# A recurrent cell on one core: the order of the second half's scan and z transpose on VectorE, and of its tanh and update gate on ScalarE

## The chip, the cores and the metric

The kernel runs on one core of one Trainium2 chip. The metric is device time in microseconds (us), the median of several runs, each of the whole program. A core has five engines that run side by side and wait for one another by semaphores: TensorE (PE, and PEld for its weight loads), VectorE (DVE), ScalarE (ACT), GpSimd (POOL) and SyncE (SP), which issues transfers.

## What is computed

A gated recurrent cell runs over T = 512 time steps for a batch of 8, with 512 inputs and 512 latent units, all in float32:

```python
def step(h, x_t):
    fused = sigmoid(concatenate([x_t, h], -1) @ w_W + w_b)
    r, z = split(fused, 2, axis=-1)                 # reset gate, update gate
    m = x_t @ wx_W + wx_b + r * (h @ wh_W + wh_b)   # memory_state
    h_new = z * h + (1.0 - z) * tanh(m)
    return h_new, h_new
out = x + scan(step, h0, x)
```

Each step needs the h of the step before, so the 512 steps form one chain.

## The kernel before

**Tiling.** The 512 latent units are KC = 4 chunks of 128 and are worked on as two halves, `o = 0` and `o = 1`, of two chunks each. On TensorE the 8 columns of h (one for each of the batch) are the stationary operand and the weights stream past, 64 columns to a product; four column tiles of 32 stand side by side. So the products of h land in PSUM with the batch on partitions and have to be turned by VectorE (`transpose` in blocks of 32) before they meet h again.

**TensorE, one step** (lines 325 to 353). The products are ordered by which half of h they need: `r(0)`, `m(0)`, `z(0, 0)` take the first half of h and wait for `h_ready[0]` (line 327); then `products_of_parts(0)` (bf16 thirds of h, which make r and m of the second half in one bank, "rm"); then line 339 waits for `h_ready[1]`, and `r(1)`, `m(1)`, `z(0, 1)` follow (48 products), `products_of_parts(1)` (24), which ends with `rm_done`, `z(1, 0)` and `z(1, 1)` (32 products, ended by `z_done[1]`), and last 8 wide products of x for a later step, `x_products` (line 265), which depend on no h of this step.

**VectorE, one step** (`step`, lines 468 to 501), in the order in which its queue takes them: turn r, m and z of the first half (434, 437, 444); `mix_m(0)`, a scan that makes r * m + x (453); `turn_rm` (441) after `rm_done`; `sum_parts(0)` (447), which gives r of the second half; `mix_h(0)`, the scan that makes the first half of the new h (461); `sum_parts(1)` (447), which gives m of the second half and signals `m_summed`; `turn_z(1)` (444), which signals `z_turned[1]`; `mix_m(1)` (453), which waits for `r_ready[1]`, `x_moved` and `m_summed` (490 to 492) and signals `m_pre_ready[1]`; `mix_h(1)` (461), which waits for `tanh_ready[1]` and `z_ready[1]` and signals `h_ready[1]`. After every fourth step a 384-wide `add_bias` follows (466).

**ScalarE, one step** (lines 384 to 405): sigmoid of r (368), sigmoid of z (375, `update(0)`), tanh (381, `new(0)`), all of the first half; the copy `put_first` (357) that puts biases and x products into PSUM for the next step; sigmoid of the second half's r (372), `put_rm` (361); then `update(1)` (375), `new(1)` (381), and `put_z` (365).

**GpSimd, one step** (lines 573 to 583): `x_moved` (576), the two subtractions that cut each half of the new h into bf16 thirds and end in `parts_ready` (544, 546), and the sum of h and x for the output (554). SyncE only moves x, the partial products `ahead` and the output.

The order on each engine is written out by hand. Every engine takes its instructions in that order, and a wait holds back all that stands behind it on the same engine.

Of the kernel before, what the change touches and what calls it, by code (L numbers as in the profile page):

```python
# [14 lines left out]
def build(nc, x, h0, w_h, w_x, b_x, b_h, x_rows, out):  # L15
# [49 lines left out]
    with ctx:  # L65
# [6 lines left out]
        def halves(name):  # L72
            return [sem(f"{name}{o}") for o in range(HALVES)]
# [82 lines left out]
        z_done = halves("z_done")  # L156
# [3 lines left out]
        z_turned = halves("z_turned")  # L160
# [10 lines left out]
        z_ready = halves("z_ready")  # L171
        m_pre_ready = halves("m_pre_ready")
        tanh_ready = halves("tanh_ready")
# [9 lines left out]
        def held(eng, value):  # L183
            return value if isinstance(value, int) else eng.snap(value)
# [169 lines left out]
        @block.scalar  # L354
        def _(act):
            def put_first(slot, t):
                act.activation(ps[:, 0:GATES, 0:W], ahead[:, slot, t, 0:GATES * W].rearrange("p (g n) -> p g n", n=W),  # L357
                               ACT.Copy).then_inc(first_ahead, 1)

            def put_rm(slot, t):  # L360
                act.activation(ps[:, RM_BANK, 0:2 * W], ahead[:, slot, t, RM_AT:COLS], ACT.Copy).then_inc(rm_ahead, 1)  # L361

            def put_z(slot, t):
                at = Z_AT[1]
                act.activation(ps[:, Z_BANK[1], 0:W], ahead[:, slot, t, at:at + W], ACT.Copy).then_inc(z_ahead, 1)

            def reset_first():
                act.activation(m_by[:, 0, :, 1].rearrange("p (c b) -> p c b", b=B), turned_r[:, :, 0:B], ACT.Sigmoid)\  # L368
                    .then_inc(r_ready[0], 1)

            def reset_second():
                act.activation(m_by[:, 1, :, 1], summed[:, 0, :, 0], ACT.Sigmoid).then_inc(r_ready[1], 1)  # L372

            def update(o):
                act.activation(h_by[:, o, :, 2].rearrange("p (b c) -> p c b", c=HC), turned_z[:, o, :, 0:B], ACT.Sigmoid)\  # L375
                    .then_inc(z_ready[o], 1)

            def new(o, s):
                n_twice = h[:, (s - 1) % RING, o, 1:1 + REGION].rearrange("p (b c w) -> p c b w", c=HC, w=TRI)[:, :, :, 0::2]
                pre = m_pre[:, o, :, 1].rearrange("p (c b) -> p c b", b=B)  # L380
                act.activation(n_twice, pre.unsqueeze(3).to_broadcast([P, HC, B, 2]), ACT.Tanh)\  # L381
                    .then_inc(tanh_ready[o], 1)

            def step(i, t0, s):
                nxt = held(act, t0 + (s + 1))
                slot, t = (s + 1) // RING % SLOTS, (s + 1) % RING
                if t == 0:
                    turn = held(act, (i * (PER_BLOCK // SLOTS) + ((s + 1) // RING // SLOTS + 1)) * LANDED)
                act.wait_ge(r_turned, nxt)
                reset_first()  # L390
                act.wait_ge(z_turned[0], nxt)
                update(0)
                act.wait_ge(m_pre_ready[0], nxt)
                new(0, s)
                if t == 0:
                    act.wait_ge(ahead_loaded[slot], turn)
                put_first(slot, t)
                act.wait_ge(r_summed, nxt)
                reset_second()
                put_rm(slot, t)  # L400
                act.wait_ge(z_turned[1], nxt)
                update(1)
                act.wait_ge(m_pre_ready[1], nxt)
                new(1, s)
                put_z(slot, t)

            act.dma_start(bias_x[:, :], b_x).then_inc(bias_x_loaded, 16)
            act.dma_start(bias_h[:, :, :], b_h).then_inc(bias_h_loaded, 16)
            act.dma_start(h_0[:, :, :], h0).then_inc(h0_loaded, 16)
            act.wait_ge(start_h, 1)  # L410
            act.activation(warm[:, :], h[:, 0, 0, 0:Q], ACT.Sigmoid)
            act.wait_ge(x_biased, 1)
            act.wait_ge(bias_h_put, HALVES)
            put_ahead(act, 0, 16)
            for k in range(KC):
                act.wait_ge(rest_once, k + 1)
                act.activation(w_parts[:, k, 1], w_rest[:, k], ACT.Copy).then_inc(second_cut, 1)  # L417
            for k in range(KC):
                act.wait_ge(rest_twice, k + 1)
                act.activation(w_parts[:, k, 2], w_rest[:, k], ACT.Copy).then_inc(third_cut, 1)  # L420
            act.wait_ge(bits_set, 1)
            act.wait_ge(ahead_loaded[0], LANDED)
            put_first(0, 0)
            put_rm(0, 0)
            put_z(0, 0)
            with nc.Fori(0, BLOCKS, engines=(mybir.EngineType.Activation,), hint_back_edge=True) as i:
                t0 = act.snap(i * STEPS)
                for s in range(STEPS):
                    step(i, t0, s)

        @block.vector
        def _(dve):
            def turn_r():
                return dve.transpose(turned_r[:, :, :], ps[:, R_BANK, 0:W].rearrange("p (c q) -> p c q", q=Q))  # L434

            def turn_m():
                return dve.transpose(turned_m.rearrange("p g (c b) w -> p c g w b", b=B),  # L437
                                     ps[:, M_BANK, 0:W].rearrange("p (c q) -> p c q", q=Q))

            def turn_rm():  # L440
                return dve.transpose(turned_rm[:, :, :], ps[:, RM_BANK, 0:2 * W].rearrange("p (c q) -> p c q", q=Q))  # L441

            def turn_z(o):
                return dve.transpose(turned_z[:, o], ps[:, Z_BANK[o], 0:W].rearrange("p (c q) -> p c q", q=Q))  # L444
# [6 lines left out]
            def mix_m(o, add):  # L451

                return dve.tensor_tensor_scan(m_pre[:, o].rearrange("p i w -> p (i w)"),  # L453
                                              m_by[:, o].rearrange("p i w -> p (i w)"),
                                              add.rearrange("p i w -> p (i w)"), 0.0, ALU.mult, ALU.add)

            def mix_h(o, s, nxt):

                dve.wait_ge(tanh_ready[o], nxt)
                dve.wait_ge(z_ready[o], nxt)  # L460
                dve.tensor_tensor_scan(h[:, s % RING, o, 0:REGION], h_by[:, o].rearrange("p i w -> p (i w)"),  # L461
                                       h[:, (s - 1) % RING, o, 1:1 + REGION], 0.0, ALU.mult, ALU.add)\
                    .then_inc(h_ready[o], 1)
# [4 lines left out]
            def step(i, t0, s):  # L468
                nxt = held(dve, t0 + (s + 1))
                dve.wait_ge(r_done, nxt)  # L470
                if s % 2 == 0:

                    dve.wait_ge(y_added, held(dve, t0 + (s + STEPS - RING + 2)))
                turn_r().then_inc(r_turned, 1)
                dve.wait_ge(m_done, nxt)
                turn_m().then_inc(m_turned, 1)
                dve.wait_ge(z_done[0], nxt)
                turn_z(0).then_inc(z_turned[0], 1)
                dve.wait_ge(r_ready[0], nxt)
                dve.wait_ge(m_turned, nxt)  # L480
                mix_m(0, turned_m[:, 0]).then_inc(m_pre_ready[0], 1)
                dve.wait_ge(rm_done, nxt)
                turn_rm().then_inc(rm_turned, 1)
                dve.wait_ge(rm_turned, nxt)
                sum_parts(0).then_inc(r_summed, 1)
                mix_h(0, s, nxt)
                sum_parts(1).then_inc(m_summed, 1)
                dve.wait_ge(z_done[1], nxt)
                turn_z(1).then_inc(z_turned[1], 1)
                dve.wait_ge(r_ready[1], nxt)  # L490
                dve.wait_ge(x_moved, nxt)
                dve.wait_ge(m_summed, nxt)
                mix_m(1, summed[:, 1]).then_inc(m_pre_ready[1], 1)
                mix_h(1, s, nxt)
                if s % RING == RING - 1:

                    g = s // RING
                    dve.wait_ge(x_product, held(dve, i * PER_BLOCK + (g + 3)))
                    dve.wait_ge(ahead_loaded[(g + 1) % SLOTS],
                                held(dve, (i * (PER_BLOCK // SLOTS) + ((g + 1) // SLOTS + 1)) * LANDED))  # L500
                    add_bias(X_BANK)
# [138 lines left out]
```

## Time and profile before

| what | value |
|---|---|
| median of 3 runs | 1635.45 us (1634.96 to 1636.28) |
| the profiled execution | 1634.35 us, of which the trace's span is 1632.2 us |
| mean granted TensorE clock | 0.995 of full speed |
| PE busy | 1603.5 us (98%) |
| DVE busy | 1162.8 us (71%) |
| ACT busy | 910.0 us (56%) |
| POOL busy | 682.3 us (42%) |
| steps | 512, so 3.1 us each |

The profile is that of one execution. "Busy" is the time in which an engine has an instruction under way. TensorE's records overlap (its matmuls are pipelined, and their ends are modelled), so there the distance from one start to the next tells more than the durations. The same is true, in a smaller way, on VectorE and ScalarE: an instruction's record may begin before the record ahead of it has ended.

### The profile page before, as it was taken

Reading aid. Unit: us, or ns where it says so; the run is one execution under the profiler, and the core shown is the slowest. Engines: PE = TensorE matmul, PEld = TensorE weight load, DVE = VectorE, ACT = ScalarE, POOL = GpSimd, SP = SyncE. Lnnn points to the kernel's source line nnn. Section 1 sums busy time; section 2 is a strip of 40 time slices with the busy share of each in tenths; the row PEclk is TensorE's granted clock in tenths of the full one; section 3 lists DMA queues with packets and bytes.
Section 4 is the critical chain, followed back from the end, with each engine's and each line's share of the span. In section 5 each row is a group of like instructions: output and inputs, shape, how many; then the busy total and the mean of one; then the engine's idle time right before and its main releaser. Section 6 shows DMA issues by size and latency. Waiting matters only on the chain.

```text
span 1632.2 us, 213115 instructions
## 1 busy us (share of the span) xinstructions
PE 1603.5 (98%) x94336; PEld 1377.4 (84%) x94336; DVE 1162.8 (71%) x5782; ACT 910.0 (56%) x4621; POOL 682.3 (42%) x3084
## 2 busy tenths in 40 slices
PE   5899999999999999999999999999999999999998
PEld 3788888888888888888888888888888888888887
DVE  3677777777777777777777777777777777777776
ACT  2455555555555555555555555555555555555555
POOL 1344444444444444444444444444444444444443
PEclk7999999999999999999999999999999999999999
DMA  6111111111111111111111111111111111111111
GB/s 203 31 51 48 52 37 49 47 53 50 47 39 51 49 47 54 37 47 52 51 48 48 40 50 47 52 51 47 39 50 50 47 53 38 48 52 50 49 47 41
DMA packets 194891, 83.29 MB, mean 51 GB/s; under 512 B 123200, under 2 KB 194368, under 8 KB 194880
## 3 DMA queue, kind: packets, MB, share of 16 engines
q1 hardware_dynamic: 193824, 82.47, 18.7%
q10 hardware_dynamic: 1056, 0.67, 0.2%
q8 instruction: 6, 0.10, 0.0%
q14 instruction: 5, 0.04, 0.0%
HBM read 49.30 MB, written 33.75 MB: 51 GB/s over the span
## 4 chain that ended last, share of the span: by engine, by line
PE 97%; DMA 1%; issue 0%; ACT 0%; ACTq 0%; DVE 0%; SPq 0%; POOL 0%; POOLq 0%; DVEq 0%
PE ps L274 56%; PE ps L283 21%; PE ps L265 20%; DMA wx<-in_w_x 1%; DMA x_rows<-xs_biased 0%; ACTq L198 0%; ACT w_parts L417 0%; ACTq L194 0%; ACT w_parts L420 0%; SPq L211 0%; SPq L209 0%; DVE xs_biased L466 0%; DVE h L461 0%; DVE turned_rm L441 0%; POOL y L554 0%
## 5 line engine op out<-in xcount | busy, mean ns | idle before, releaser
L274 PE MATMUL ps<-wh,h 128*8 128x64 f32 x65536 | 1218.0, 219 | 20.0 <-ACT ps L357 14.6
L274 PEld LDWEIGHTS ps<-wh,h 128*8 128x8 f32 x65536 | 1030.9, 92 | 238.8 <-DVE h L461 216.4
L283 PE MATMUL ps<-w_parts,h 128*24 128x128 bf16 x24576 | 544.1, 219 | 0.0
L283 PEld LDWEIGHTS ps<-w_parts,h 128*24 128x24 bf16 x24576 | 442.8, 121 | 0.0
L265 PE MATMUL ps<-wx,x_grp 128*32 128x384 f32 x4096 | 430.7, 486 | 0.0
L368 ACT ACTIVATE m_by<-turned_r 128x16 f32<-128x16 f32 x512 | 112.0, 219 | 561.4 <-DVE turned_r L434 561.4
L544 POOL TENSOR_TENSOR h<-h 128x16 f32<-128x16 f32 x1026 | 224.4, 219 | 365.5 <-DVE h L461 361.9
L461 DVE TENSOR_TENSOR_SCAN h<-h_by,h 128x48 f32<-128x48 f32 x1024 | 260.6, 254 | 160.9 <-ACT h L381 160.9
L576 POOL TENSOR_TENSOR summed<-turned_rm,nothing 128x16 f32<-128x16 f32 x512 | 113.5, 222 | 498.6 <-DVE turned_rm L441 498.6
L434 DVE STREAM_TRANSPOSE turned_r<-ps 128x64 f32<-128x64 f32 x512 | 128.1, 250 | 262.9 <-PE ps L274 258.4
L375 ACT ACTIVATE h_by<-turned_z 128x16 f32<-128x16 f32 x1024 | 238.5, 233 | 117.9 <-DVE turned_z L444 63.2
L546 POOL TENSOR_TENSOR h<-h 128x16 f32<-128x16 f32 x1026 | 225.0, 219 | 80.4
L381 ACT ACTIVATE h<-m_pre 128x32 f32<-128x32 f32 x1024 | 252.7, 247 | 0.0
L444 DVE STREAM_TRANSPOSE turned_z<-ps 128x64 f32<-128x64 f32 x1024 | 247.9, 242 | 2.9 <-PE ps L274 2.9
L447 DVE TENSOR_REDUCE summed<-turned_rm 128x16 f32<-128x48 f32 x1024 | 197.1, 192 | 17.4
L357 ACT ACTIVATE ps<-ahead 128x192 f32<-128x192 f32 x513 | 171.6, 335 | 0.0
L441 DVE STREAM_TRANSPOSE turned_rm<-ps 128x128 f32<-128x128 f32 x512 | 162.1, 317 | 0.3 <-PE ps L283 0.3
L554 POOL TENSOR_TENSOR y<-x_sb,h 128x32 f32 x512 | 137.9, 269 | 0.9
L361 ACT ACTIVATE ps<-ahead 128x128 f32<-128x128 f32 x513 | 135.1, 263 | 0.0
L437 DVE STREAM_TRANSPOSE turned_m<-ps 128x64 f32<-128x64 f32 x512 | 119.5, 233 | 1.5 <-PE ps L274 1.4
L372 ACT ACTIVATE m_by<-summed 128x16 f32<-128x16 f32 x512 | 112.1, 219 | 14.5 <-DVE summed L447 0.4
L453 DVE TENSOR_TENSOR_SCAN m_pre<-m_by,summed 128x32 f32<-128x32 f32 x512 | 115.0, 225 | 0.0
(29 smaller groups left out, 429.4 us busy)
## 6 DMA issues: line engine op xcount, KB each, us to landing
x_rows<-xs_biased SPq DMA_DIRECT2D x128, 192.0 KB, 1.9
ahead<-x_rows SPq DMA_DIRECT2D x512, 32.0 KB
ahead<-x_rows SPq DMA_DIRECT2D x1024, 8.0 KB
x_sb<-in_x SPq DMA_DIRECT2D x34, 256.0 KB, 3.1
x_grp<-in_x SPq DMA_DIRECT2D x516, 16.0 KB, 1.7
out_h<-y SPq DMA_DIRECT2D x32, 256.0 KB, 2.7
wx<-in_w_x SPq DMA_DIRECT2D x4, 768.0 KB, 9.1
wh<-in_w_h SPq DMA_DIRECT2D x4, 512.0 KB, 7.3
```

Source lines behind the costliest of these rows:

```text
L265: mm = pe.matmul(ps[Q * j:Q * (j + 1), bank, 0:COLS], stands, wx[:, k, j, :], start=(k == 0), stop=(k == KC - 1), tile_position=(0, Q * j))
L274: mm = pe.matmul(ps[Q * j:Q * j + B, bank, 0:W], h_of(s - 1, k), wh[:, k, j, at:at + W], start=False, stop=(k == KC - 1), skip_group_check ...
L283: mm = pe.matmul(ps[Q * j:Q * j + PARTS * B, RM_BANK, 0:2 * W], parts_of(s - 1, k), w_parts[:, k, part, j], start=False, stop=(k == KC - 1 ...
L357: act.activation(ps[:, 0:GATES, 0:W], ahead[:, slot, t, 0:GATES * W].rearrange("p (g n) -> p g n", n=W), ACT.Copy).then_inc(first_ahead, 1)
L375: act.activation(h_by[:, o, :, 2].rearrange("p (b c) -> p c b", c=HC), turned_z[:, o, :, 0:B], ACT.Sigmoid)\
L381: act.activation(n_twice, pre.unsqueeze(3).to_broadcast([P, HC, B, 2]), ACT.Tanh)\
L441: return dve.transpose(turned_rm[:, :, :], ps[:, RM_BANK, 0:2 * W].rearrange("p (c q) -> p c q", q=Q))
L444: return dve.transpose(turned_z[:, o], ps[:, Z_BANK[o], 0:W].rearrange("p (c q) -> p c q", q=Q))
L447: return dve.tensor_reduce(summed[:, g, :, 0].rearrange("p (c b) -> p c b", b=B), turned_rm[:, HC * g:HC * (g + 1)].rearrange("p c (w b) - ...
L461: dve.tensor_tensor_scan(h[:, s % RING, o, 0:REGION], h_by[:, o].rearrange("p i w -> p (i w)"), h[:, (s - 1) % RING, o, 1:1 + REGION], 0.0 ...
L544: pool.tensor_tensor(mid(1, s, o), mid(0, s, o), mid_top(0, s, o), ALU.subtract).then_inc(left_once[o], 1)
L546: pool.tensor_tensor(mid(2, s, o), mid(1, s, o), mid_top(1, s, o), ALU.subtract)\
```

## The change

It moves one instruction on each of two engines and swaps two waits. On VectorE, `mix_m(1)` with its three waits now stands directly behind `sum_parts(1)`, and `turn_z(1)` with its wait for `z_done[1]` behind `mix_m(1)`. On ScalarE, the second half's tanh `new(1)` with its wait for `m_pre_ready[1]` now stands ahead of the sigmoid `update(1)` with its wait for `z_turned[1]`. In `mix_h(1)` the wait for `z_ready[1]` is now written first and that for `tanh_ready[1]` second; `mix_h(0)` keeps its order. No instruction is added, removed or resized, and TensorE, GpSimd and SyncE have the same code.

```diff
@@ ScalarE step
                 put_rm(slot, t)
+                act.wait_ge(m_pre_ready[1], nxt)
+                new(1, s)
                 act.wait_ge(z_turned[1], nxt)
                 update(1)
-                act.wait_ge(m_pre_ready[1], nxt)
-                new(1, s)
                 put_z(slot, t)
@@ VectorE mix_h(o, s, nxt)
-                dve.wait_ge(tanh_ready[o], nxt)
-                dve.wait_ge(z_ready[o], nxt)
+                for ready in ((tanh_ready[o], z_ready[o]), (z_ready[o], tanh_ready[o]))[o]:
+                    dve.wait_ge(ready, nxt)
@@ VectorE step
                 sum_parts(1).then_inc(m_summed, 1)
-                dve.wait_ge(z_done[1], nxt)
-                turn_z(1).then_inc(z_turned[1], 1)
                 dve.wait_ge(r_ready[1], nxt)
                 dve.wait_ge(x_moved, nxt)
                 dve.wait_ge(m_summed, nxt)
                 mix_m(1, summed[:, 1]).then_inc(m_pre_ready[1], 1)
+                dve.wait_ge(z_done[1], nxt)
+                turn_z(1).then_inc(z_turned[1], 1)
                 mix_h(1, s, nxt)
```

## Rows read from the trace of the kernel before

**Rows 1.** The page's chain that ended last: its shares by engine.
```profile
PE 97%; DMA 1%; issue 0%; ACT 0%; ACTq 0%; DVE 0%; SPq 0%; POOL 0%; POOLq 0%; DVEq 0%
```

**Rows 2.** Waits from 60 to 1600 us: who waited for whom, total us, times, longest.
```profile
PEld ps L274 <- DVE h L461: 211.5, 497, 0.4
DVE h L461 <- ACT h L381: 155.9, 496, 0.3
```

**Rows 3.** Timeline, PE: start us, us, engine, line, operation, idle before.
```profile
802.17 0.76 PEld L274 LDWEIGHTS ps<-wh,h 128*8 128x8 f32 x48 [0.42 <-DVE h L461]
802.25 0.87 PE L274 MATMUL ps<-wh,h 128*8 128x64 f32 x48
...
802.87 0.43 PEld L283 LDWEIGHTS ps<-w_parts,h 128*24 128x24 bf16 x24
...
803.21 0.73 PEld L274 LDWEIGHTS ps<-wh,h 128*8 128x8 f32 x48
...
803.87 0.43 PEld L283 LDWEIGHTS ps<-w_parts,h 128*24 128x24 bf16 x24
803.93 0.53 PE L283 MATMUL ps<-w_parts,h 128*24 128x128 bf16 x24
...
804.21 0.52 PEld L274 LDWEIGHTS ps<-wh,h 128*8 128x8 f32 x32
```

**Rows 4.** Timeline of the same step, DVE and ACT, the second half's work.
```profile
801.75 0.21 DVE L447 TENSOR_REDUCE summed<-turned_rm 128x16 f32<-128x48 f32 x1
...
801.87 0.25 DVE L461 TENSOR_TENSOR_SCAN h<-h_by,h 128x48 f32<-128x48 f32 x1
801.99 0.22 ACT L372 ACTIVATE m_by<-summed 128x16 f32<-128x16 f32 x1
802.04 0.18 DVE L447 TENSOR_REDUCE summed<-turned_rm 128x16 f32<-128x48 f32 x1
...
802.14 0.23 DVE L444 STREAM_TRANSPOSE turned_z<-ps 128x64 f32<-128x64 f32 x1
...
802.35 0.23 DVE L453 TENSOR_TENSOR_SCAN m_pre<-m_by,summed 128x32 f32<-128x32 f32 x1
802.41 0.23 ACT L375 ACTIVATE h_by<-turned_z 128x16 f32<-128x16 f32 x1
...
802.61 0.25 ACT L381 ACTIVATE h<-m_pre 128x32 f32<-128x32 f32 x1
...
802.89 0.26 DVE L461 TENSOR_TENSOR_SCAN h<-h_by,h 128x48 f32<-128x48 f32 x1 [0.32 <-ACT h L381]
```

**Rows 5.** Timeline, the same reduce and scan one step on.
```profile
805.15 0.18 DVE L447 TENSOR_REDUCE summed<-turned_rm 128x16 f32<-128x48 f32 x1
...
805.46 0.23 DVE L453 TENSOR_TENSOR_SCAN m_pre<-m_by,summed 128x32 f32<-128x32 f32 x1
```

**Rows 6.** Timeline, DVE alone, an early step: z's transpose came late, all else was ready.
```profile
40.08 0.25 DVE L444 STREAM_TRANSPOSE turned_z<-ps 128x64 f32<-128x64 f32 x1 [1.11 <-PE ps L274]
...
40.25 0.18 DVE L453 TENSOR_TENSOR_SCAN m_pre<-m_by,summed 128x32 f32<-128x32 f32 x1
```

**Rows 7.** Timeline, DVE, the first half's transposes and scan, then the next transpose.
```profile
804.00 0.21 DVE L437 STREAM_TRANSPOSE turned_m<-ps 128x64 f32<-128x64 f32 x1
804.11 0.22 ACT L368 ACTIVATE m_by<-turned_r 128x16 f32<-128x16 f32 x1 [1.13 <-DVE turned_r L434]
804.18 0.25 DVE L444 STREAM_TRANSPOSE turned_z<-ps 128x64 f32<-128x64 f32 x1
804.36 0.23 DVE L453 TENSOR_TENSOR_SCAN m_pre<-m_by,turned_m 128x32 f32<-128x32 f32 x1
...
804.50 0.32 DVE L441 STREAM_TRANSPOSE turned_rm<-ps 128x128 f32<-128x128 f32 x1
```

**Rows 8.** Lines from 60 to 1600 us: busy us, mean ns | idle before.
```profile
L444 DVE STREAM_TRANSPOSE turned_z<-ps 128x64 f32<-128x64 f32 x994 | 240.5, 242 | 0.0
L375 ACT ACTIVATE h_by<-turned_z 128x16 f32<-128x16 f32 x994 | 231.5, 233 | 109.6 <-DVE turned_z L444 56.2
```

## The prediction

> **What bounds the kernel now.** I read the chain that ended last first. It gives PE 97% [rows 1], so TensorE, which looks busy without a break, sets the time. Work that is moved between VectorE and ScalarE can then gain only what TensorE loses by waiting, and can cost whatever makes TensorE wait. So the question is how close each half of h arrives to the moment at which TensorE wants it. The waits name both places. The weight loads waited 211.5 us, 497 times, for the scan of line 461 [rows 2]: that is the first half, once a step. But it is PEld that waits; the wide x products run on meanwhile, and r(0)'s first matmul begins 0.08 us after its load (802.17 to 802.25), against 0.06 at the start of the parts block at 803.87 [rows 3]. The first half of h thus has a few hundredths of slack.
>
> The second half is what the change touches. Its scan on line 461 begins at 802.89 and lasts 0.26, so it ends at 803.15 [rows 4], and the load for r(1) begins at 803.21 [rows 3], 0.06 later. Is that load held up by h, or by the 24 loads ahead of it? From the first of those loads to the load of r(1) it is 802.87 to 803.21 = 0.34, and the same block of the other half, which has no h to wait for behind it, also takes 803.87 to 804.21 = 0.34 [rows 3]. So h's second half arrives just as TensorE is ready for it. A gain on it buys at most 0.01 us a step, the resolution of these rows, hence 5 us in 512 steps. A loss is paid nearly in full, since this is a loop: r(1), m(1), z(0,1) and parts(1) lead to `rm_done`, that to VectorE's turning and sums, and these to the second half of the next h. With that loop exactly as long as TensorE's own step, any time added on it lengthens every step.
>
> **What ends the second half now.** From the timeline [rows 4]: the sum of m, 802.04 + 0.18 = 802.22; the transpose of z, 802.14; the scan of m, 802.35; the sigmoid of z, 802.41; tanh, 802.61; the scan of h, 802.89. The last link is tanh (802.86), 0.03 ahead of that scan, and the waits say the same: line 461 waited for line 381 496 times, 155.9 us [rows 2]. Sigmoid ended at 802.64, 0.22 us earlier. From the start of the scan of m to the start of the scan of h it is 802.89 - 802.35 = 0.54.
>
> **The change part by part.** All 512 steps have it; nothing is added.
>
> 1. The scan of m is put ahead of the transpose of z. How much earlier does it begin? By the order of the queue alone, VectorE could give it 0.10 to 0.21. But its inputs bound it: r's sigmoid ends at 801.99 + 0.22 = 802.21 and the sum of m at 802.22 [rows 4]. The best case is 0.03 behind the latter, 802.25, as the scan of h follows tanh: 0.10 earlier. The worst is that nothing is gained. I choose the worst, from this: the scan begins 0.13 behind the end of that sum, and one step later again 805.15 + 0.18 = 805.33 to 805.46 = 0.13 [rows 4, 5]. The transpose between them doesn't explain this. Where everything else had long been ready, the same scan began 0.17 behind the transpose (40.08 to 40.25) [rows 6]; here it is 802.14 to 802.35 = 0.21, and its record is 0.23 long instead of 0.18 [rows 4, 6], as that of the scan at 804.36, which came just as its sigmoid ended (804.33) [rows 7]. So it is not queueing behind the transpose; it is being released late, and its releaser is the sum. It has three waits, and `m_summed` is the last in the code. As I read the 0.13, that wait has to pass by itself before the scan is taken up, and this costs the 0.10 over the 0.03. That path (sum, wait, scan) is the same in the changed kernel. The scan stays at 802.35, or moves by 0.02.
>
> The Trainium skill, "Perfetto Trace Analysis", section "Identifying Dependency Chains", says that an instruction with several waits may have separate wait instructions put ahead of it, and "Advanced Engine Details and Errata", "Network/Comms", gives 50-100 ns for a sequencer on TRN2 to read a semaphore. The 0.10 between 0.13 and 0.03 in the rows is of that size; no row shows such an instruction by itself.
>
> 2. The transpose of z now follows the scan. It was ready long before (z(1,1) is on TensorE ahead of the x products), so only the queue holds it. Spacing on VectorE: 0.14 behind a 0.23 scan of this form (804.36 to 804.50) [rows 7], where the next also waited for TensorE's block at 803.93 + 0.53 = 804.46 [rows 3], so 0.14 is an upper end; the lower is 0.10, as the transpose behind the 0.18 sum [rows 4]. I take 0.14, as records that overlap lie about 0.08 less than the duration apart in both pairs (0.18 and 0.10; 0.25 and 0.18 at 804.18 [rows 4, 7]). It lasts 0.23 [rows 4] to 0.25 [rows 7]; mean 0.242 [rows 8]. I take 0.24.
>
> 3. The sigmoid of z comes 0.04 behind the transpose's end (802.37 to 802.41), lasts 0.233, and the scan of h follows by 0.03 [rows 4, 8]. Tanh starts where it does now, 802.61, so ScalarE is free for the sigmoid in good time, though their records overlap. Behind the sigmoid, line 365's copy is later by as much; what it fills is wanted by z(1,0), at 804.2 + the delay, more than a microsecond on.
>
> 4. The swapped waits of `mix_h(1)`: the late one is again the one written first (tanh before, now z), so I take the same 0.03, not the 0.13 of the scan of m. In the code that is all that the swap does.
>
> **The sum.** From the start of the scan of m to that of h: 0.14 + 0.24 + 0.04 + 0.23 + 0.03 = 0.68, against 0.54 now: 0.14 later. Tanh, 0.22 late behind sigmoid now, is no longer the last; z is. Less 0.01 or nothing of slack: 0.13 a step. 512 x 0.13 = 66.6 us, on the profiled 1634.35: 1701.0. The median stands 1.1 above the profiled execution, so 1702 us, 4.1% slower. Ends: 0.10 + 0.23 + 0.03 + 0.23 + 0.03 = 0.62, with the scan 0.02 earlier and 0.01 slack, adds 0.05, 26 us (1661); 0.14 + 0.25 + 0.04 + 0.24 + 0.04 = 0.71 adds 0.17, 87 us (1722); these need all errors at once, so 1680 to 1716 for the case alone.
>
> Nothing else takes it back: TensorE's delayed r(1) delays `rm_done`, and every engine's step with it; GpSimd's cut of the second half starts from the same scan and shifts equally. SyncE's transfers are not on the path.
>
> **Rivals.**
> - *The scan of m does start 0.10 earlier*, at 802.25. For it: its inputs allow this. Against it: the 0.13 twice over and the long record. Then 0.14 - 0.10 = 0.04, less slack 0.03 to 0.04: 15 to 20 us, 1652.
> - *The chain of z is longer still*: the transpose starts only when the scan has ended (0.23 instead of 0.14), or the scan of h pays 0.10 for its late wait. 0.23 a step, 118 us: 1753. Against: 0.17 and 0.18 between 0.25 records [rows 6, 7]. The Trainium skill, "VectorE: DVE Perf Modes", "The DRAIN you can't avoid", has a next operation wait until the pipe is empty; the rows show overlap, as its own section on instructions with no wait between them allows.
> - *No change*, 1636: h's second half has 0.14 of slack that I don't see, since TensorE's ends are modelled. Against: its load starts 0.06 behind the end of the scan (803.15), and that of the first half, which is known to wait, 0.05 behind its own (801.87 + 0.25 = 802.12) [rows 3, 4].
> - *Faster*, the other side: the scan of m comes more than 0.15 earlier (the transpose sets its release after all, and the sum's signal comes ahead of its recorded end). It decides from a scan of m at 802.20: then 0.68 behind it is 802.88, before today's 802.89, and TensorE gets at most its 0.01 a step, 5 us: 1630. But 802.20 lies ahead of both inputs as recorded.
> - *TensorE's clock falls* in the new pauses of 0.13 us; it is 0.995 of the full 2.4 GHz on average with the present ones. At 1.2 GHz a step's 3.1 us of matmuls would double. I see no row for it.
>
> **How the numbers follow.** Forecast case 0.75, scan earlier 0.12, longer chain 0.04, no change 0.04, faster 0.04, clock 0.01. The range takes the forecast's own 1680 to 1716 and reaches down over the first rival, 1650 to 1716. About 0.2% is what a measurement of this kernel can tell from no change, so faster 0.04, same 0.04, slower 0.92.
>
> **What would show it.** In the changed trace: line 461 waits for line 375 instead of 381, 512 times; the scan of m still 0.13 behind the end of the sum; the transpose 0.14 behind the scan's start; the scan of h 0.68 behind it; a gap of 0.13 ahead of r(1) on PE and PEld, with a step of 3.23 us in place of 3.10; PE's share of the last chain down, with DVE and ACT in it. A scan of m 0.03 behind the sum would make it the first rival, an unbroken TensorE the third.

## The result, and the profile after

The changed kernel takes 1678.07 us (median of 5, 1677.77 to 1679.15), the kernel before 1635.45 (median of 5, 1634.52 to 1636.28). The ratio is 1.026, 95% interval 1.025 to 1.027: 42.6 us slower, or 42.6 / 512 = 0.083 us a step. The forecast was 1702, within 1650 to 1716.

| | before | after |
|---|---|---|
| profiled execution, its span | 1634.35, 1632.2 us | 1678.07, 1676.2 us |
| mean granted TensorE clock | 0.995 | 0.995 |
| PE busy | 1603.5 us | 1646.0 us |
| DVE busy | 1162.8 us | 1161.8 us |
| ACT busy | 910.0 us | 871.4 us |

The page of the changed kernel still gives nearly everything to TensorE. Its chain that ended last, shares by engine:

```profile
PE 97%; DMA 1%; issue 0%; ACT 0%; ACTq 0%; DVE 0%; SPq 0%; POOL 0%; DVEq 0%; POOLq 0%
```

That is the same 97% as in [rows 1], in a kernel that is slower although TensorE's instructions are the same. The prediction had expected the share to fall; it doesn't, so a share of 97% can't tell whether TensorE waits a little in every step. It falls only to 92% in `e3` and 91% in `e2` (below), where the block of r(1) comes on average 0.15 and 0.20 us later behind the one ahead of it than in the kernel before. The waits from 60 to 1640 us do show what has changed (total us, times, longest):

```profile
DVE h L461 <- ACT h_by L375: 149.1, 496, 0.3
ACT h L381 <- DVE m_pre L453: 121.7, 496, 0.4
```

The scan of h waited for tanh, line 381, in [rows 2]; now it waits for the sigmoid of z, line 375. And ScalarE stands idle ahead of tanh, since the sigmoid that used to fill this time is behind it. One step of the changed kernel, VectorE and ScalarE, answering to [rows 4]:

```profile
800.94 0.21 DVE L447 TENSOR_REDUCE summed<-turned_rm 128x16 f32<-128x48 f32 x1
...
801.24 0.18 DVE L447 TENSOR_REDUCE summed<-turned_rm 128x16 f32<-128x48 f32 x1
...
801.55 0.22 DVE L453 TENSOR_TENSOR_SCAN m_pre<-m_by,summed 128x32 f32<-128x32 f32 x1
...
801.70 0.22 DVE L444 STREAM_TRANSPOSE turned_z<-ps 128x64 f32<-128x64 f32 x1
801.81 0.25 ACT L381 ACTIVATE h<-m_pre 128x32 f32<-128x32 f32 x1 [0.24 <-DVE m_pre L453]
801.95 0.23 ACT L375 ACTIVATE h_by<-turned_z 128x16 f32<-128x16 f32 x1
...
802.22 0.26 DVE L461 TENSOR_TENSOR_SCAN h<-h_by,h 128x48 f32<-128x48 f32 x1 [0.30 <-ACT h_by L375]
```

The scan of m begins 801.55 - 801.42 = 0.13 behind the end of the sum, exactly as before: moving it ahead of the transpose gained nothing. The transpose of z is pushed from ahead of the scan to 0.15 behind its start, and z is now last: from the scan of m to the scan of h 0.67 us, against 0.54. TensorE in the same step, answering to [rows 3]:

```profile
802.08 0.42 PEld L283 LDWEIGHTS ps<-w_parts,h 128*24 128x24 bf16 x24
802.13 0.52 PE L283 MATMUL ps<-w_parts,h 128*24 128x128 bf16 x24
...
802.53 0.69 PEld L274 LDWEIGHTS ps<-wh,h 128*8 128x8 f32 x48
802.53 0.86 PE L274 MATMUL ps<-wh,h 128*8 128x64 f32 x48
...
803.21 0.52 PE L283 MATMUL ps<-w_parts,h 128*24 128x128 bf16 x24
```

From the first load of the parts block to the first load of r(1) it is 0.45 us, against 0.34 before, and between their first matmuls 0.40 (802.13 to 802.53), against 0.34 (802.92 to 803.26): that is the pause. Averaged over the steps from 60 to 1600 us the distance between these first matmuls is 0.409 us against 0.335, and that from r(1) to `products_of_parts(1)` 0.680 against 0.670: together the 0.08 a step that the change costs. The other four distances between blocks are the same in both kernels. The second thing to see is that r(1)'s first matmul starts together with its load (both 802.53). In the kernel before it started 0.05 behind it (803.21 in [rows 3]; the matmul is the last row below, from the timeline of that kernel). The load used to run 0.05 ahead of a matmul that still had other matmuls in front of it. That lead is the cover that the prediction did not count, and it is why the pause in this step is 0.11 between loads and 0.06 between matmuls. The kernel before, PE, in order `products_of_parts(1)`, z(1, 0) and z(1, 1), x, `products_of_parts(0)` and r(1):

```profile
800.83 0.53 PE L283 MATMUL ps<-w_parts,h 128*24 128x128 bf16 x24
801.16 0.64 PE L274 MATMUL ps<-wh,h 128*8 128x64 f32 x32
...
801.61 0.84 PE L265 MATMUL ps<-wx,x_grp 128*32 128x384 f32 x8
...
802.92 0.53 PE L283 MATMUL ps<-w_parts,h 128*24 128x128 bf16 x24
...
803.26 0.87 PE L274 MATMUL ps<-wh,h 128*8 128x64 f32 x48
```

### The profile page after: what moved, and what is told of

It reads as the page before. It is cut to its first block, busy times and chain, and to the rows that moved or that the text cites. A ratio compares the mean times of both kernels' runs of the same rounds, so it can differ in the third digit from the quotient of the medians.

```text
span 1676.2 us, 213115 instructions
## 1 busy us (share of the span) xinstructions
PE 1646.0 (98%) x94336; PEld 1396.8 (83%) x94336; DVE 1161.8 (69%) x5782; ACT 871.4 (52%) x4621; POOL 682.2 (41%) x3084
## 4 chain that ended last, share of the span: by engine, by line
PE 97%; DMA 1%; issue 0%; ACT 0%; ACTq 0%; DVE 0%; SPq 0%; POOL 0%; DVEq 0%; POOLq 0%
PE ps L274 57%; PE ps L283 20%; PE ps L265 20%; DMA wx<-in_w_x 1%; DMA x_rows<-xs_biased 0%; ACTq L198 0%; ACT w_parts L417 0%; ACT w_parts L420 0%; ACTq L194 0%; SPq L211 0%; SPq L209 0%; DVE xs_biased L466 0%; DVE h L461 0%; DVE m_pre L453 0%; DVE turned_rm L441 0%
## 5 line engine op out<-in xcount | busy, mean ns | idle before, releaser
L274 PE MATMUL ps<-wh,h 128*8 128x64 f32 x65536 | 1205.4, 220 | 20.3 <-ACT ps L357 14.3
L274 PEld LDWEIGHTS ps<-wh,h 128*8 128x8 f32 x65536 | 997.4, 92 | 262.3 <-DVE h L461 224.0
L283 PE MATMUL ps<-w_parts,h 128*24 128x128 bf16 x24576 | 532.0, 219 | 0.0
L283 PEld LDWEIGHTS ps<-w_parts,h 128*24 128x24 bf16 x24576 | 431.3, 121 | 0.0
L265 PE MATMUL ps<-wx,x_grp 128*32 128x384 f32 x4096 | 425.4, 487 | 0.0
L444 DVE STREAM_TRANSPOSE turned_z<-ps 128x64 f32<-128x64 f32 x1024 | 242.3, 237 | 3.2 <-PE ps L274 3.2
```

Source lines behind the costliest of these rows:

```text
L265: mm = pe.matmul(ps[Q * j:Q * (j + 1), bank, 0:COLS], stands, wx[:, k, j, :], start=(k == 0), stop=(k == KC - 1), tile_position=(0, Q * j))
L274: mm = pe.matmul(ps[Q * j:Q * j + B, bank, 0:W], h_of(s - 1, k), wh[:, k, j, at:at + W], start=False, stop=(k == KC - 1), skip_group_check ...
L283: mm = pe.matmul(ps[Q * j:Q * j + PARTS * B, RM_BANK, 0:2 * W], parts_of(s - 1, k), w_parts[:, k, part, j], start=False, stop=(k == KC - 1 ...
```

## The experiments

The working measure is one distance, read on VectorE: from the start of the first line-447 sum (of r, second half) to the start of the second half's scan of h. In the kernel before it is 1.15 us on average (1.14 in the step of [rows 4], 801.75 to 802.89). How much a kernel lengthens it, the delay, is compared with what a step costs, the difference of medians over 512.

### Each half of the change alone

`e1_scalar_only`: ScalarE's order and the swapped waits; VectorE as before.

```diff
                 put_rm(slot, t)
+                act.wait_ge(m_pre_ready[1], nxt)
+                new(1, s)
                 act.wait_ge(z_turned[1], nxt)
                 update(1)
-                act.wait_ge(m_pre_ready[1], nxt)
-                new(1, s)
```

> ScalarE's part alone: tanh ahead of the sigmoid of z, and the swapped waits of the scan of h; VectorE in the order of before. The scan of m stays 0.13 behind the sum, tanh starts where it did, the sigmoid 0.13 behind it: the scan of h 0.11 later. Theory A (0.05 of cover): 0.06 a step, 33 us, 1669. Theory B (0.01): 51 us, 1687.

Measured: 1663.5 us, ratio 1.018 (1.016 to 1.019), 28.5 us slower. The sigmoid of z, which ran 0.06 behind the start of the scan of m in [rows 4], now stands behind tanh and runs 0.40 behind it:

```profile
800.04 0.23 DVE L453 TENSOR_TENSOR_SCAN m_pre<-m_by,summed 128x32 f32<-128x32 f32 x1
...
800.30 0.25 ACT L381 ACTIVATE h<-m_pre 128x32 f32<-128x32 f32 x1 [0.23 <-DVE m_pre L453]
800.44 0.22 ACT L375 ACTIVATE h_by<-turned_z 128x16 f32<-128x16 f32 x1
...
800.69 0.26 DVE L461 TENSOR_TENSOR_SCAN h<-h_by,h 128x48 f32<-128x48 f32 x1 [0.42 <-ACT h_by L375]
```

ScalarE's new order costs on its own: with only that, 0.65 us from scan to scan.

`e2_vector_only`: VectorE's order; ScalarE and the waits as before.

```diff
                 sum_parts(1).then_inc(m_summed, 1)
-                dve.wait_ge(z_done[1], nxt)
-                turn_z(1).then_inc(z_turned[1], 1)
 ...
                 mix_m(1, summed[:, 1]).then_inc(m_pre_ready[1], 1)
+                dve.wait_ge(z_done[1], nxt)
+                turn_z(1).then_inc(z_turned[1], 1)
```

> VectorE's part alone: the scan of m ahead of z's transpose; ScalarE and the waits of the scan of h as before. Tanh has to stand behind the sigmoid of z, which waits for the late transpose: scan of h 0.29 later. Theory A: 0.24 a step, 123 us, 1758. Theory B: 0.28, 143 us, 1779. If the scan of m came 0.10 earlier through the move, both would be 51 us less.

Measured: 1742.7 us, ratio 1.066 (1.064 to 1.067), 107.6 us slower, more than the whole change. Tanh, whose input is ready, has to stand behind a sigmoid that waits for the late transpose. So VectorE's part is the larger loss, and ScalarE's part is what repairs most of it; together they cost 42.6. The delay was 0.25 rather than the 0.29 worked out. Neither half gains anything.

### The two waits of the scan of h

`e3_old_waits`: the changed kernel, tanh's wait written first again.

```diff
-                for ready in ((tanh_ready[o], z_ready[o]), (z_ready[o], tanh_ready[o]))[o]:
-                    dve.wait_ge(ready, nxt)
+                dve.wait_ge(tanh_ready[o], nxt)
+                dve.wait_ge(z_ready[o], nxt)
```

> The changed kernel, with the waits of the second scan of h in their old order (tanh written first, z second), so that the late one is the second. If the late wait costs 0.10 more where it is not the one written first, as the 0.13 behind the sum of m suggests: 51 us more than the changed kernel, 1729. If the order of the two waits means nothing: 1678.

Measured: 1714.1 us, ratio 1.049 (1.047 to 1.050), 36 us more than the changed kernel. The order in which two waits are written matters: the late one is cheap where it is written first.

```profile
801.92 0.23 ACT L375 ACTIVATE h_by<-turned_z 128x16 f32<-128x16 f32 x1
...
802.26 0.26 DVE L461 TENSOR_TENSOR_SCAN h<-h_by,h 128x48 f32<-128x48 f32 x1 [0.37 <-ACT h_by L375]
```

The scan starts 0.11 behind the sigmoid's end (802.15), in the changed kernel 0.04 (802.18 to 802.22). The price is 0.07 and 36 / 512 = 0.07 a step, not the 0.10 that I took from the scan of m.

### The three waits of the scan of m

`e4_after_joined`: the changed kernel, the three signals counted on one semaphore. `e5_before_joined`: the same in the kernel before.

```diff
+                all_three = held(dve, t0 * 3 + 3 * (s + 1))
 ...
-                sum_parts(1).then_inc(m_summed, 1)
+                sum_parts(1).then_inc(r_ready[1], 1)
-                dve.wait_ge(r_ready[1], nxt)
-                dve.wait_ge(x_moved, nxt)
-                dve.wait_ge(m_summed, nxt)
+                dve.wait_ge(r_ready[1], all_three)
 ...                # GpSimd's move of x
-                        .then_inc(x_moved, 1)
+                        .then_inc(r_ready[1], 1)
```

> The changed kernel, with the three signals that the scan of m of the second half waits for counted on one semaphore and waited for once (the sum of m's value, 3 for each step). If the 0.13 between the end of the sum and the scan is the price of the late wait that stands by itself: the scan starts 0.03 behind the sum, the scan of h 0.10 earlier than in the changed kernel, about 0.04 later than in the kernel before, inside TensorE's cover of 0.05 (theory A): 1635 to 1640. With 0.01 of cover (theory B): 1650. If the 0.13 is not the wait's: 1678.

Measured: 1635.4 us, ratio 1.000 (0.999 to 1.001): the whole loss is gone, with both new orders in place. VectorE in one step:

```profile
800.71 0.18 DVE L447 TENSOR_REDUCE summed<-turned_rm 128x16 f32<-128x48 f32 x1
...
800.93 0.24 DVE L453 TENSOR_TENSOR_SCAN m_pre<-m_by,summed 128x32 f32<-128x32 f32 x1
...
801.60 0.26 DVE L461 TENSOR_TENSOR_SCAN h<-h_by,h 128x48 f32<-128x48 f32 x1 [0.30 <-ACT h_by L375]
```

The scan now starts 0.04 behind the end of the sum (800.89), not 0.13, and the rest is unchanged (0.67 from scan to scan). So 0.09 of the 0.13 was the price of the late wait. The transpose didn't hold the scan back: in the changed kernel it stands behind the scan, and the 0.13 is there all the same.

The separate wait is itself in the traces, though the timeline leaves it out. The records of two lines of waits, kernel before (count, shortest, median and longest in ns, first and last start in us):

```profile
L492 DVEq EVENT_SEMAPHORE  x512: 49/50/50, 35.6 to 1627.3; - x171
L460 DVEq EVENT_SEMAPHORE  x1024: 21/21/21, 35.1 to 1627.7; - x171
```

By the semaphores recorded with them, the wait written first (`r_ready[1]`) is on the scan of m itself, and the other two, `x_moved` and `m_summed`, are this one instruction ahead of it. Averaged over the steps, it begins 0.04 behind the end of the sum and lasts 0.05, and the scan begins 0.04 behind its end: 0.13 in all. In `e4` there is no such instruction ahead of the scan of m. Line 460 is the second wait of both scans of h, with one signal, and lasts 0.02; in `e3` it begins 0.04 behind the sigmoid's end and the scan 0.04 behind it, 0.10 in all, where a wait on the scan itself takes 0.03. That is the 0.07 of `e3`, and why it is less than the 0.09 here. Three separate waits with `m_summed` written first were not tried.

> Kernel before, with the scan of m of the second half waiting once, on one semaphore that counts all three signals. The second half's h comes 0.04 to 0.07 us earlier. If the kernel before is bound by TensorE's own work or by the loop through the first half of h: the same, within 3 us of 1635. If the loop through the second half is as long as the step (as predicted, Theory B): up to 5 us faster, or more if TensorE isn't full.

Measured: 1635.3 us, ratio 1.000 (0.999 to 1.001). The distance falls from 1.15 to 1.06, so the second half of h is 0.09 earlier, and the time doesn't move. The loop through the second half is not what sets the step of the kernel before. Here the transpose still stands ahead, and the scan of m begins 0.09 behind the sum; but it lasts 0.18 instead of 0.24 and ends 0.27 behind the sum (802.18 to 802.45), in `e4` 0.28 (800.89 to 801.17). At the end of the scan the transpose makes no difference either.

### How much delay is free

`e6_one_spare` and `e7_two_spare`: the kernel before with one or two spare copies between the sigmoid of z and tanh.

```diff
                 update(1)
+                act.activation(spare[:, 0:1], warm[:, 0:1], ACT.Copy)
+                act.activation(spare[:, 1:2], warm[:, 1:2], ACT.Copy)    # e7 alone
                 act.wait_ge(m_pre_ready[1], nxt)
                 new(1, s)
```

> Kernel before, with one spare one-column copy on ScalarE between the second half's sigmoid of z and its tanh, so that tanh and with it the second half's h come some 0.03 to 0.05 us later in each step. Theory A (TensorE has about 0.05 us of cover: r(1)'s first matmul stands behind the parts block, not behind h): within 3 us of the kernel before. Theory B (as predicted: 0.01 of cover): 0.03 a step, 12 to 20 us slower.

Measured: 1635.6 us, ratio 1.000 (0.999 to 1.001). It tells nothing about the cover: the spare copy ran while ScalarE was waiting for the scan of m, and the distance stayed 1.15. What I had expected to be a delay was none.

> The same with two spare copies: tanh some 0.13 us later than in the kernel before, about what the change does to the second half's h. Theory A: 0.13 - 0.05 = 0.08 a step, 41 us slower, 1676, next to the changed kernel. Theory B: 0.12 a step, 61 us slower, 1697.

Measured: 1657.0 us, ratio 1.013 (1.012 to 1.015), 21.7 us slower. The distance is 1.24, a delay of 0.09 instead of 0.13, so neither theory's time can be compared as it stands; but 0.09 of delay cost only 21.7 / 512 = 0.042. About 0.05 of it was free, where theory B allowed 0.01. `e4` shows the same from the other side: its h is 0.04 later at no cost, and the load of r(1) is only 0.01 ahead of its matmul (801.92 to 801.93), where it was 0.05.

`e12_h0_late`: the kernel before with a spare copy on VectorE ahead of the scan of the first half of h, which makes both halves later.

```diff
                 sum_parts(0).then_inc(r_summed, 1)
+                dve.tensor_copy(spare[:, 0:1], nothing[:, 0, 0:1])
                 mix_h(0, s, nxt)
```

> Kernel before, with a spare one-column copy on VectorE ahead of the scan of the first half of h, which makes both halves of h some 0.06 us later. Theory F (no cover on the first half, 0.05 on the second): the whole delay is paid, 0.06 a step, about 30 us slower. If the first half too has cover, 0.03 by the 0.08 between r(0)'s load and its matmul: 15 us. If TensorE's own work alone sets the step: nothing.

Measured: 1642.4 us, ratio 1.004 (1.003 to 1.006), 7.2 us slower, 0.014 a step.

```profile
802.67 0.21 DVE L448 TENSOR_REDUCE summed<-turned_rm 128x16 f32<-128x48 f32 x1
...
802.80 0.14 DVE L487 COPY spare<-nothing 128x1 f32<-128x1 f32 x1
802.86 0.25 DVE L462 TENSOR_TENSOR_SCAN h<-h_by,h 128x48 f32<-128x48 f32 x1
...
803.88 0.26 DVE L462 TENSOR_TENSOR_SCAN h<-h_by,h 128x48 f32<-128x48 f32 x1 [0.32 <-ACT h L382]
```

The first half's scan is 0.19 behind the sum's start, against 0.12 (801.75 to 801.87, [rows 4]); the second half's 1.21, against 1.15. Both halves are about 0.06 later and 0.014 is paid. Theory F, that the loop through the first half is as long as the step, falls: that half has cover too, 0.05 at least. The load of r(0) is now 0.03 ahead of its matmul (803.16 to 803.19), against 0.08 in [rows 3].

### TensorE's own work

`e8_before_3_tiles` and `e9_after_3_tiles`: the x products of one of the four column tiles left out, in the kernel before and the changed one.

```diff
-                    last = x_products(s, x_grp[:, s, :])
+                    last = x_products(s, x_grp[:, s, :], tiles=TILES - 1)
```

> Kernel before, with the x products of one of the four column tiles left out in the loop (so a quarter of the values of x @ W is missing from the gates): 0.16 us less work on TensorE in each step. Theory A: TensorE's own work sets the step, but the loops through h are only 0.03 to 0.05 shorter: 15 to 26 us faster, 1610 to 1620. Theory C (only TensorE's work counts, the loops have much cover): 0.16 a step, 82 us faster. Theory B (the loop through h's second half is as long as TensorE's step): 0 to 5 us.

> The changed kernel with the same x products left out. Theories A and B: the loop through h's second half sets the step now and holds no x products, so it stays within 3 us of the changed kernel, 1678. Theory C (TensorE's work still counts in each step): up to 82 us faster than that, 1596.

Measured: 1635.2 us, ratio 1.000 (0.999 to 1.001), and 1678.0, ratio 1.026 (1.025 to 1.028): each as its kernel. But these two don't test what they were made for. TensorE in the first of them:

```profile
802.73 0.84 PE L265 MATMUL ps<-wx,x_grp 128*32 128x384 f32 x6
803.32 0.89 PE L274 MATMUL ps<-wh,h 128*8 128x64 f32 x46
...
804.05 0.53 PE L283 MATMUL ps<-w_parts,h 128*24 128x128 bf16 x23
```

Six records take 0.84 us, and eight took 0.84 in the kernel before (801.61, in its timeline). The products of the four column tiles run side by side, so the three that remain take as long. I had counted a quarter of 0.65 us as saved; next to none of it was. The first matmul of r(0) does start 0.59 behind the first x product instead of 0.64, but the next block, all but its first matmul, starts 1.32 behind it (802.73 to 804.05), against 1.31 (801.61 to 802.92) before. Nothing about theory C follows, nor about the others.

`e10_h0_first`: `e5` with the first half's scan of h ahead of the sum of r, and the wait for the output's sum ahead of that for r's products. `e11_h0_first_3_tiles` leaves out the same x products besides.

```diff
+                mix_h(0, s, nxt)
                 dve.wait_ge(rm_turned, nxt)
                 sum_parts(0).then_inc(r_summed, 1)
-                mix_h(0, s, nxt)
```

> The one-semaphore kernel before, with the scan that makes the first half of h ahead of the sum of r of the second half (h's first half 0.12 earlier, the second half's 0.03 later, inside its 0.05 of cover), and the wait for the output's sum written ahead of that for r's products (0.08 less on the alternate steps' first half). Theory F (the loop through the first half of h sets the step of the kernel before, and TensorE's own work is a little less): 0.01 to 0.03 a step, 5 to 15 us faster. If TensorE's own work is as long as that loop: the same.

Measured: 1658.1 us, ratio 1.013 (1.012 to 1.015), slower by 22.8. The first half did come early, but TensorE could not use it, and the second half came later than I had worked out:

```profile
801.14 0.86 PEld L274 LDWEIGHTS ps<-wh,h 128*8 128x8 f32 x48 [0.32 <-DVE h L461]
...
801.34 0.85 PE L274 MATMUL ps<-wh,h 128*8 128x64 f32 x48
```

The load of r(0) starts when h's first half is there, and its first matmul 0.20 later, behind the x products (0.08 in [rows 3]). So TensorE's queue, not the first half of h, decides when r(0) begins. The second half's scan of h is 1.60 behind the start of `turn_rm` (800.47 to 802.07), against 1.49 (801.40 to 802.89) before: 0.11 later instead of 0.03, because the sum of r starts 0.18 later, where 0.12 was counted; from there to the scan of h it is 1.07, as in `e5` (1.06). The second half's loop then sets the step. The four runs spread more than those of the other kernels (1655.5 to 1664.4), and the execution with the trace is the longest of them.

> The kernel with the first half's scan first, and with the x products of one column tile left out in the loop (a quarter of the values of x @ W missing from the gates), 0.16 less work for TensorE. Theory F: leaving them out gained nothing in the kernel before because the loop through the first half of h was as long; with that loop 0.12 shorter it gains until the second half's loop is met, 0.02 to 0.05 a step: 10 to 25 us faster than before, 1610 to 1625. If the second half's loop or something else binds both: 1635.

Measured: 1661.8 us, ratio 1.016 (1.015 to 1.018), as `e10` within what the runs of the two spread over. As with `e8`, leaving the tile out frees next to nothing, and the second half's loop binds in any case.

### All kernels on one line

| kernel | distance, us | delay | cost a step | delay less cost |
|---|---|---|---|---|
| e5 | 1.06 | -0.09 | 0.000 | |
| before | 1.15 | 0 | 0 | |
| e6 | 1.15 | 0.00 | 0.001 | |
| e4 | 1.19 | 0.04 | 0.001 | 0.04 |
| e12 | 1.21 | 0.06 | 0.014 | 0.05 |
| e7 | 1.24 | 0.09 | 0.042 | 0.05 |
| e1 | 1.25 | 0.10 | 0.056 | 0.04 |
| e10, the execution with the trace | (1.60 from turn_rm) | 0.11 | 0.057 | 0.05 |
| after | 1.28 | 0.13 | 0.083 | 0.05 |
| e3 | 1.35 | 0.20 | 0.154 | 0.05 |
| e2 | 1.40 | 0.25 | 0.210 | 0.04 |

Whatever makes the second half of h later, on VectorE or on ScalarE, by an order, a wait or a spare instruction, the first 0.04 to 0.05 us are free and the rest is paid in full. For `e10` the cost is that of the execution from which its delay is read, (1664.39 - 1635.23) / 512; by the median it is 0.045. The delays in the table are read from one step, to 0.01 us. Averaged over the steps from 60 to 1600 us, the delay less the growth of the step is 0.049 to 0.050 us in all seven slower kernels.

## Why the prediction was right, and where its size was off

**The scan of m gains nothing: right.** It was put at 0.13 behind the end of the sum, and is there in the changed kernel; `e4` shows the cause that was only argued then (0.13 becomes 0.04 when one wait is left). The prediction said that no row shows a wait instruction by itself; line 492 of the kernel before is one. The first rival, a scan that starts 0.10 earlier, fell, although its inputs allowed it.

**z's chain becomes the last: right.** The waits name line 375 in place of line 381. The sum gave 0.68 from scan to scan; it measures 0.67: 0.15 to the transpose (0.14 taken), 0.22 for the transpose (0.24), 0.03 to the sigmoid (0.04), 0.23 for it, and 0.04 to the scan (0.03). Against 0.54 that is 0.13, where 0.14 was forecast. The rival of a longer chain fell too: the transpose overlaps the scan, and the late wait, written first, costs 0.04. With the waits unswapped it would have been that rival in part (`e3`).

**The cover of the second half: wrong, and this is the miss.** "A loss is paid nearly in full" rested on "the second half arrives just as TensorE is ready for it", with 0.01 of slack. The experiments give 0.05. The reading compared loads with loads: 0.34 us for the parts block in both halves. It did not look at the matmul behind the load. For the first half I did, and allowed a few hundredths; for the second the same 0.05 stood between 803.21 and 803.26, and a late load first eats up this lead. Of the 24 us between 1702 and 1678, (0.13 - 0.083) x 512, the cover makes some 19 and the shorter chain 5. The rival "no change" had the right mechanism, with 0.14 of cover where there is 0.05.

**"TensorE sets the time": right, though the 97% didn't show it.** The step of the kernel before shrinks neither when the second half of h comes 0.09 earlier (`e5`), nor is it set by the loop through the first half (`e12`, 0.06 later at 0.014, all of which the second half accounts for). In `e10` r(0) waits 0.20 behind its load for the x products. The distances between the first matmuls of TensorE's blocks say it directly: from 800.83 to 803.93, 0.33, 0.45, 0.64, 0.67, 0.34 and 0.67, which is the whole step of 3.10. Those ahead of the two blocks that wait for h don't shrink when h comes earlier: on average 0.335 ahead of r(1) in `e5` too, and 0.645 ahead of r(0) in `e10` too. So there is no pause to win there. What no run shows is how far the step falls when TensorE has less to do: `e8` took away nothing that counts, and a narrower x product in all four tiles wasn't tried.

**TensorE's clock** stayed at 0.995 with the longer pauses, so that rival fell. The wait for `z_ahead` behind the later copy of line 365 never showed.

**A version that beats both** did not come out. `e4` and `e5` bring the second half of h earlier and equal the kernel before, which has no use for it. What `e4` is good for is that the new orders, costly as they are with three waits, cost nothing with one.

## What to carry to other kernels

Moving an instruction forward in a queue gains only if the queue held it: compare its start with the end of each of its inputs first, here 0.13 behind the sum, with or without the transpose between. The instruction that it jumps over then pays, and if that one's chain (transpose, sigmoid) is nearly as long, it becomes the last. When several waits stand ahead of one instruction, write the late one first or count the signals on one semaphore, and read the cover of a consumer from its matmul, not from its weight load.

## What the runs showed of the hardware

- On VectorE the wait written first is on the instruction itself, and the others are a separate one ahead of it, 0.02 us long with one signal (line 460) and 0.05 with two (line 492). A late wait among those costs 0.07 us (`e3`: 0.11 against 0.04 behind the sigmoid) to 0.09 us (`e4` against the changed kernel: 0.13 and 0.04 behind the sum). The Trainium skill, "Perfetto Trace Analysis", section "Identifying Dependency Chains", says that an instruction that waits for several engines may have wait instructions put ahead of it for the further conditions. The traces agree with that, and line 460 is one where both waits are for the same engine, ScalarE.
- A load may run 0.05 us ahead of its matmul, and with a full queue in front it does (0.05 ahead of r(1) in the kernel before, 0.00 in the changed one); 0.05 us of lateness of the operand are free in all seven slower kernels of the table.
- Three column tiles' products take as long as four's (0.84 us for six records and for eight).
- The same 32-element scan lasted 0.28 us in `e10`, 0.23 in the kernel before and 0.18 in `e5`. What makes the record longer was not tried.
